# A routed two-layer network after attention: results added to the output rows tile by tile instead of in a last stage

## The reference

```
x      = x + attention(layernorm(x), ctx)
flat   = layernorm(x)                                   # rows the experts read
scores = softmax(flat @ router_weight.T + router_bias)  # T x 8
topk_vals, topk_idx = top_k(scores, 2)                  # two experts a token
gu     = flat @ gate_up_proj[e] + gate_up_bias[e]       # 512 -> 1024
gate   = minimum(gu[:512], 7);  up = clip(gu[512:], -7, 7)
act    = (up + 1) * gate * sigmoid(1.702 * gate)
down   = act @ down_proj[e] + down_bias[e]              # 512 -> 512
out    = x + sum over the token's two experts of topk_val * down
```

## Time and profile before

| | |
|---|---|
| median of 3 runs | 2001.87 us (1999.96 to 2002.34) |
| profiled execution, its own time | 2003.26 us |
| its span | 2001.5 us |
| mean granted TensorE clock | 0.933 of full speed |
| PE busy in the span | 1726.6 us (86%) |
| DVE busy | 1337.1 us (67%) |
| ACT busy | 667.1 us (33%) |
| POOL busy | 373.7 us (19%) |
| indirect gathers `xg` | 78 |
| indirect gathers `ya` | 64 |

### The profile page before, as it was taken

One profiled execution on the slowest core, in us unless ns is written; L12 is line 12 of the kernel. 1 busy time (PEld: TensorE's weight loads), 2 busy tenths in 40 slices (PEclk: granted clock), 3 DMA queues, 4 the chain that ended last, 5 costly groups with the idle time before them and its releaser, 6 DMA issues. The chain is left out here.

```text
span 2001.5 us, 31191 instructions
## 1 busy us (share of the span) xinstructions
PE 1726.6 (86%) x10594; PEld 1248.7 (62%) x10594; DVE 1337.1 (67%) x2380; ACT 667.1 (33%) x1108; POOL 373.7 (19%) x543
## 2 busy tenths in 40 slices
PE   6989999999899999998996389999999999999600
PEld 4547456365474563654743379898988988989500
DVE  3776776757767667577675766767677677776444
ACT  2341542623415326234153232424244244332100
POOL 3113013021130130211310111111111111110165
PEclk9999999999999999999998589999999999999855
DMA  6405216034062160340511413434354254421388
GB/s 213 115 1 167 67 38 195 2 89 144 1 170 64 39 194 2 96 138 1 148 44 43 169 32 106 150 104 148 108 178 159 96 190 155 162 85 54 116 290 297
DMA packets 111380, 228.70 MB, mean 114 GB/s; under 512 B 21232, under 2 KB 22256, under 8 KB 111216
## 3 DMA queue, kind: packets, MB, share of 16 engines
q1 hardware_dynamic: 85472, 162.40, 24.8%
q0 software_dynamic: 20576, 54.29, 9.3%
q10 hardware_dynamic: 5168, 9.96, 1.3%
HBM read 208.59 MB, written 45.61 MB: 127 GB/s over the span
## 5 line engine op out<-in xcount | busy, mean ns | idle before, releaser
L1205 PE MATMUL gu_ps<-xgT_hi,wg_hi 128*128 128x256 f32 x1248 | 356.3, 286 | 41.7 <-issue 40.1
L1205 PE MATMUL gu_ps<-xgT_hi,wg_lo 128*128 128x256 f32 x1248 | 353.8, 283 | 0.0
L1205 PE MATMUL gu_ps<-xgT_lo,wg_hi 128*128 128x256 f32 x1248 | 353.6, 283 | 0.0
L448 ACT ACTIVATE pt<-st 128x1024 f32<-128x1024 f32 x256 | 249.3, 1018 | 152.2 <-PE st L291 152.2
L1205 PEld LDWEIGHTS gu_ps<-xgT_hi,wg_hi 128*128 128x128 f32 x1248 | 243.2, 195 | 51.8 <-issue 51.2
L1205 PEld LDWEIGHTS gu_ps<-xgT_lo,wg_hi 128*128 128x128 f32 x1248 | 243.3, 195 | 0.7
L1205 PEld LDWEIGHTS gu_ps<-xgT_hi,wg_lo 128*128 128x128 f32 x1248 | 242.9, 195 | 0.0
L609 DVE TENSOR_REDUCE negmax<-work 128x1 f32<-128x512 f32 x256 | 174.9, 689 | 62.5 <-PE work L276 61.4
L1320 DVE TENSOR_SCALAR gate<-gu_ps,bg 128x256 f32<-128x256 f32 x156 | 75.3, 482 | 165.1 <-PE gu_ps L1205 165.1
L291 PE MATMUL st<-qs,ks 98*128 98x512 f32 x512 | 165.2, 416 | 5.9 <-ACT pt L448 5.2
L609 DVE TENSOR_REDUCE negmax<-st 128x2 f32<-128x1024 f32 x128 | 151.6, 1218 | 25.6 <-PE st L276 23.9
(11 more groups left out here) (174 smaller groups left out, 3023.1 us busy)
## 6 DMA issues: line engine op xcount, KB each, us to landing
raw_g<-w_gate_up SPq DMA_DIRECT2D x39, 2048.0 KB
raw_d<-w_down SPq DMA_DIRECT2D x39, 1024.0 KB
ks<-k_hi SPq DMA_DIRECT2D x256, 64.0 KB, 2.0
qs<-q_hi SPq DMA_DIRECT2D x256, 64.0 KB, 2.4
y_dram<-y SPq DMA_DIRECT2D x20, 512.0 KB, 3.2
bd<-b_down SPq DMA_DIRECT2D x39, 256.0 KB
y_dram<-y ACTq DMA_DIRECT2D x19, 512.0 KB, 2.8
x_in<-x SPq DMA_DIRECT2D x8, 1024.0 KB, 5.4
```

The lines of the kernel that those rows point to most:

```text
L448: e.activation(pt[k % 2][:, 2 * p:2 * p + 2, :], st[st_ring.bank[b, "exp", c, k, p]][:, :, :], ACT.Exp, scale=scale).then_inc(exped.sem, 1)
L1205: ins = e.matmul(gu_ps[n % GU_BANKS][:, part, :], wg[s][pw][:, k, cols], xgT[s][px][:, k, :], start=(k == 0 and m == 0), stop=(k == KD - 1 ...
```

## The change

- `combine_stage` is gone, with `y_dram`, `x2_dram`, `w12` and the `y` and `hid_f` tiles. The attention stage stores its residual rows into `out`.
- Rows of `xln_dram` get 8 more floats behind their 512: a DMA in the routing stage, first on SP's queue, writes there the token's weight for each expert (zero for those not chosen). The gather of a tile's rows brings them along, and `pick_weight` (two small VectorE instructions after `row_lo`) picks the tile's expert by `tile_hot`.
- `mix(i)` takes the place of `add_down_bias(i)`: four VectorE instructions of 128x512 (`scalar_tensor_tensor`): `acc = d_ps * w + acc` twice, then `acc = bd * w + acc` twice. It stands one turn later, after f = 1 of the next tile's parts, ahead of the `down_lo` and `gate_up_lo` there.
- GpSimd has in each turn: scatter `acc` of tile i - 1 to `out` (two indirect DMAs, each after its half is mixed), wait for them to land, fetch the rows of tile i + 3 (two), gather the rows of `out` for tile i into `acc` (two). The next `mix` waits for these.
- SP's load of the down bias waits for `mixed` of tile i; the stores of `y` on SP and ScalarE are gone.
- `hidden_lo(f - 2)` stands ahead of `clip(f)`, which now waits for it, as `hid_f` is kept in `up`.
- The routing stage has some 20 more small VectorE instructions and two matmuls after the token list, which give padding slots a token of their tile or a spare one.

```diff
@@ routing_stage
             e.wait_ge(exped, 1)
-            then(e.tensor_reduce(inv_sum[:, :], expo[:, :, :], AX.X, ALU.add))
-            last()
-            then(e.reciprocal(w12[:, 0, :], inv_sum[:, :]))
-            ...
+            then(e.tensor_reduce(exp_sum[:, :], expo[:, :, :], AX.X, ALU.add))
+            last()
+            then(e.tensor_tensor(weight[:, :, :], expo[:, :, :], hots[:, :, :], ALU.mult))
+            then(e.reciprocal(inv_sum[:, :], exp_sum[:, :]))
+            last()
+            then(e.tensor_tensor(weight[:, :, :], weight[:, :, :], e_of(inv_sum[:, :]), ALU.mult), "weight")
...
+            then(e.tensor_scalar(pad[:, :], token_1[:, :], 0.5, None, ALU.is_lt))
+            last()
+            e.wait_ge(first_sent, 1)
+            then(e.tensor_tensor(pad[:, :], pad[:, :], first_ps[:, :], ALU.mult))
+            ...
+            then(e.tensor_scalar(in_run[:, :], column(token_f, 0), part_f[:, 0:1], None, ALU.is_equal), "in_run")
+            e.wait_ge(run_made, 1)
+            ...
+            then(e.tensor_copy(token_of[:, :], token_f[:, :]))
...
         def on_sp(e):
+            e.wait_ge(vec, at["weight"])
+            e.dma_start(w_rows, weight[:, :, :]).then_inc(w_stored, 16)
             e.wait_ge(vec, at["tiles"])
             first_loads(e)
@@ expert_stage, TensorE
                         if k == 0 and i:
-                            e.wait_ge(y_made.sem, y_made[i - 1, j])
+                            e.wait_ge(y_added.sem, y_added[i - 1, j])
@@ expert_stage, VectorE
-            def add_down_bias(i):
+            def pick_weight(i):
+                e.wait_ge(gathered[i % 2], turn(i) * 16 * SUB)
+                ...
+                e.tensor_tensor(w_all[:, :, :], xg[i % 2][:, :, D:DX], tile_hot[:, i, :, :], ALU.mult).then_inc(w_made.sem, 1)
+                e.wait_ge(w_made.sem, w_made[i, "all"])
+                e.tensor_reduce(w_slot[i % WSL][:, :], w_all[:, :, :], AX.X, ALU.add).then_inc(w_made.sem, 1)
+
+            def mix(i):
                 s = i % 2
+                e.wait_ge(acc_in[s], turn(i) * 16 * SUB)
+                e.wait_ge(w_made.sem, w_made[i, "slot"])
+                for j in range(SUB):
+                    e.wait_ge(down_made.sem, down_made[i, j])
+                    e.scalar_tensor_tensor(out=acc[s][:, j, :], in0=d_ps[j][:, :], scalar=w_slot[i % WSL][:, j:j + 1], in1=acc[s][:, j, :],
+                                           op0=ALU.mult, op1=ALU.add).then_inc(y_added.sem, 1)
                 e.wait_ge(bd_in[s], turn(i) * 16)
                 for j in range(SUB):
-                    e.wait_ge(down_made.sem, down_made[i, j])
-                    if i >= 2:
-                        e.wait_ge(stored[s], 16 * (turn(i) - 1))
-                    e.tensor_tensor(y[s][:, j, :], d_ps[j][:, :], bd[s][:, :], ALU.add).then_inc(y_made.sem, 1)
+                    e.wait_ge(y_added.sem, y_added[i, j])
+                    e.scalar_tensor_tensor(out=acc[s][:, j, :], in0=bd[s][:, :], scalar=w_slot[i % WSL][:, j:j + 1], in1=acc[s][:, j, :],
+                                           op0=ALU.mult, op1=ALU.add).then_inc(mixed.sem, 1)
...
                     for f in range(KF):
+                        if f > 1:
+                            hidden_lo(now, f - 2)
                         clip(now, f)
                         if f:
                             glu(now, f - 1)
-                        if f > 1:
-                            hidden_lo(now, f - 2)
+                        if f == 1 and i >= 1:
+                            mix(i - 1)
                         if f % 2:
                             down_lo(now, f // 2, down_changed)
...
                 if i + 2 < n_tiles:
                     row_lo(i + 2)
-                if i >= 0:
-                    add_down_bias(i)
+                    pick_weight(i + 2)
+            mix(n_tiles - 2)
+            mix(n_tiles - 1)
@@ expert_stage, GpSimd
+            def fetch_sums(i):
+                s = i % 2
+                if i:
+                    e.wait_ge(scattered.sem, scattered[i - 1])
+                for j in range(SUB):
+                    e.indirect_dma_start(out=acc[s][:, j, :], out_offset=None, in_=out_rows, in_offset=slot_rows(i, j)).then_inc(acc_in[s], 16)
+
+            def store_sums(i):
+                for j in range(SUB):
+                    e.wait_ge(mixed.sem, mixed[i, j])
+                    e.indirect_dma_start(out=out_rows, out_offset=slot_rows(i, j), in_=acc[i % 2][:, j, :], in_offset=None).then_inc(scattered.sem, 16)
+
+            e.wait_ge(w_stored, 16)
             fetch(0)
             fetch(1)
-            for i in range(-1, n_tiles - 1):
+            fetch_sums(0)
+            for i in range(-1, n_tiles):
+                if i >= 1:
+                    store_sums(i - 1)
                 if i + 3 < n_tiles:
                     fetch(i + 3)
+                if i >= 1:
+                    fetch_sums(i)
+            store_sums(n_tiles - 1)
+            e.wait_ge(scattered.sem, scattered[n_tiles - 1])
@@ expert_stage, SP
                 if i >= 2:
-                    e.wait_ge(y_made.sem, y_made[i - 2, SUB - 1])
+                    e.wait_ge(mixed.sem, mixed[i - 2, SUB - 1])
```

More of the change, by code:

```diff
@@ L866, in routing_stage @@
     SLOTS = token_of.shape[1]
+    SUB = FTOK // P
     SHIFT = P.bit_length() - 1
@@ L911, in routing_stage @@
         low = sb("low", [P, SLOTS])
+        token_1 = sb("token_1", [P, SLOTS])
+        token_f = sb("token_f", [P, SLOTS])
+        pad = sb("pad", [P, SLOTS])
+        first = sb("first", [P, SLOTS])
+        empty = sb("empty", [P, n_tiles])
+        spare = sb("spare", [P, n_tiles])
+        in_run = sb("in_run", [P, n_tiles], BF16)
+        ones_row = sb("ones_row", [1, P])
         ended = sb("ended", [P, n_tiles, E])
@@ L1044, in on_dve @@
                 n_some = KT // NQ
-                tiles = slice(some.start % NT, some.start % NT + n_some)
+                tiles = slice(some.start % NT + 1, some.start % NT + n_some + 1)
                 last()
@@ L1079, in on_pe @@
             ins.then_inc(listed, 1)
+            e.wait_ge(consts_made, ONES_ROW)
+            e.wait_ge(vec, at["token_1"])
+            e.matmul(first_ps[:, :], ones_row[:, :], token_1[0:1, :], start=True, stop=True).then_inc(first_sent, 1)
+            e.wait_ge(vec, at["in_run"])
+            e.matmul(run_ps[:, :], ones_b[:, :], in_run[:, :], start=True, stop=True).then_inc(run_made, 1)
         def on_sp(e):
+            e.wait_ge(vec, at["weight"])
+            e.dma_start(w_rows, weight[:, :, :]).then_inc(w_stored, 16)
             e.wait_ge(vec, at["tiles"])
@@ L1116, in expert_stage @@
     GU_BANKS = 4
+    IDX, WSL = 4, 3
+    DX = D + E
     rows = xln_dram.rearrange("b s d -> (b s) d")
+    out_rows = out.rearrange("b s d -> (b s) d")
     tiles = range(n_tiles)
@@ L1130, in expert_stage @@
         bu1 = [sb(f"bu1{s}", [P, KF]) for s in range(2)]
-        idx = [sb(f"idx{s}", [P, SUB], I32) for s in range(2)]
-        xg = [sb(f"xg{s}", [P, SUB, D]) for s in range(2)]
+        idx = [sb(f"idx{s}", [P, SUB], I32) for s in range(IDX)]
+        xg = [sb(f"xg{s}", [P, SUB, DX]) for s in range(2)]
+        acc = [sb(f"acc{s}", [P, SUB, D]) for s in range(2)]
+        w_all = sb("w_all", [P, SUB, E])
+        w_slot = [sb(f"w_slot{s}", [P, SUB]) for s in range(WSL)]
         xgT = [pair("xgT", [P, KD, FTOK], s) for s in range(2)]
@@ L1136, in expert_stage @@
         up = [sb(f"up{i}", [P, FTOK]) for i in range(2)]
-        hid_f = [sb(f"hid_f{i}", [P, FTOK]) for i in range(2)]
         hid = [pair("hid", [P, KF, FTOK], s) for s in range(2)]
-        y = [sb(f"y{s}", [P, SUB, D]) for s in range(2)]
         t_ps = [psum(f"t_ps{i}", [P, 2, FTOK]) for i in range(KD // 2)]
@@ L1150, in expert_stage @@
         gathered = [sem(f"gathered{s}") for s in range(2)]
-        stored = [sem(f"stored{s}") for s in range(2)]
+        acc_in = [sem(f"acc_in{s}") for s in range(2)]
+        scattered = Mark(sem("scattered"), tiles, 16 * SUB)
+        w_made = Mark(sem("w_made"), [(i, n) for i in tiles for n in ("all", "slot")])
         of_f = [(i, f) for i in tiles for f in range(KF)]
@@ L1159, in expert_stage @@
         glu_made, hid_made, hid_lo_made = Mark(sem("glu_made"), of_f), Mark(sem("hid_made"), of_f), Mark(sem("hid_lo_made"), of_f)
-        y_made = Mark(sem("y_made"), [(i, j) for i in tiles for j in range(SUB)])
+        y_added = Mark(sem("y_added"), [(i, j) for i in tiles for j in range(SUB)])
+        mixed = Mark(sem("mixed"), [(i, j) for i in tiles for j in range(SUB)])
         idx_made = Mark(sem("idx_made"), tiles)
@@ L1373, in on_dve @@
             row_lo(0)
+            pick_weight(0)
             for i in range(-1, n_tiles):
@@ L1448, in on_sp @@
                     load_down_bias(i + 2)
-                if i >= 0 and i % 2 == 0:
-                    store(e, i)
-            for s in range(2):
-                e.wait_ge(stored[s], 16 * len(tiles[s::2]))
```

152 lines of the change are left out of this document (57 added, 95 removed).

## The result

The changed kernel takes 2017.83 us, the median of 4 runs (2016.04 to 2021.23); the kernel before took 2000.91 beside it. The ratio is 1.0088, 95% interval 1.007 to 1.0107: slower by 0.9%. The profiled execution took 2016.04 us; its span is 2014.3, against 2001.5 before, and its mean granted clock 0.942.

A forecast was written before the change was run, and what follows sets the result against it. It took PE to bound plain turns, VectorE's serial work turns with new weights, and GpSimd and DMA the 116 us combining stage. Terms: -103.1 + 92 + 3 + 6 + 5.7 = +3.6 us; forecast 2005 us, range 1968 to 2043.

The forecast's parts named there:

- three signs: Forecast wrong if plain turns exceed 18 us (loop), A and C don't slow the clock, or ScalarE waits for `raw_g`.
- the loop: Slower rival: GpSimd's round through DRAM (scatter, gather, landings) exceeds 17.6 us and decides; 2045 to 2053; chance 0.16.
- Routing, +5.7: Dependent steps and two PE trips behind the token list, two steps before it: 5.7 us, bounds 4 and 8.
- A, B and C: Three turns where an expert follows another: +2.75, +5.3, +3.1, turn behind C +2.0; 13.1 us, seven times: 92.
- The clock: Waits of about 3 us drop PE to the lower clock; 1.9 to 3.0 us of turn C are the clock's.
- The rival in which the clock does not follow: Faster: new waits of 2.6 to 3.8 us leave the clock alone; 8.6 a place, 1973; chance 0.24.
- The rival of late weights: Slower: weight loads share DMA engines badly, ScalarE waits in B too, 3 us at seven places: 2026; chance 0.10.
- SP: Down-bias load waits for `mixed` and delays weight loads: 1.2 us in A at five places, 6 us; B 0.
- Plain turns, the step that failed: Turns without new weights: VectorE's idle time absorbs most of `mix`; 0.3 us a turn, ten turns, 3 us.
- mix, 2.7 us: Four VectorE instructions about 0.68 apart, 2.7 us, bounds 2.6 and 3.0; serial addition with `clip`'s waits 2.9.
- GpSimd's chain, 15.5 us a round: Round from `mix` to `mix` through scatter and gather takes 15.5 us, below 17.6, so price 0.
- The end, 36.3 us: Last scatter lands 36.3 us behind the last `gate_up`, where the span ended 139.45 behind; gain 103.1 us.

The follow-up runs named there:

- the best version: Changed kernel with mix(i) behind row_lo, old order of hidden_lo and large tiles at multiples of 64 bytes: 1911.77 us, ratio 0.9566; with filling 1898.43 us, ratio 0.9488.
- the filling: Best version plus 14 identity matmuls whose result nobody reads ahead of gate_up of turn C, seven places: 1898.43 us, ratio 0.9488.
- The run with half the filling: Changed kernel plus 14, 24 and 10 identity matmuls ahead of gate_up behind turns A, B and C, seven places: 2013.18 us, ratio 1.005.
- the bias run: Changed kernel with SP's load of the down bias moved behind the weight loads: 2021.28 us, ratio 1.0097.
- without both: Changed kernel with half the filling and SP's down-bias loads behind the weight loads, both at once: 1985.45 us, ratio 0.9924.
- The order run: Changed kernel with hidden_lo(f - 2) back behind glu(f - 1) and its own hid_f tile, mix left in place: 2016.15 us, ratio 1.0074.
- the late `mix`: Changed kernel with mix(i) at the end of turn i, behind row_lo and pick_weight: 1923.32 us, ratio 0.9628.
- half a `mix` less: Changed kernel with the second pair of mix instructions (weighed down bias) left out: 1993.51 us, ratio 0.9948.
- the first aligned kernel: Changed kernel plus two unused 32-byte tiles, so every large expert-stage tile starts at a multiple of 64 bytes: 2016.52 us, ratio 1.0086.

## Why the prediction came out as it did

The forecast for the profiled execution was +3.6 us; it was +12.8, in the range (which was 75 us wide) and on the side that had the most weight, but outside the forecast's no change. That it came so near is in part luck: the steps below miss by 18.3 us on one side and by 9 on the other. The prediction also named three signs by which it would be wrong, and two of them came, the third in part. Plain turns are over 18 us, though not by the loop that the sign stood for; four of the seven C leave the clock alone; and ScalarE waits for `raw_g`, 30.7 us in seven waits, which the prediction's own term for late weights in A had foreseen, so that this sign contradicted the sum. By its steps:

*Routing, +5.7.* The first `gate_up` starts 5.4 later. Right.

*A, B and C.* The seven A grew by 26.0 us, forecast 23.2 (2.75 each, and 2.0 for the two that stand behind a C); B by 35.2, forecast 37; C by 20.6, forecast 22. The waits behind them were forecast at 3.8, 6 and 2.6 us and are 4.20, 6.26 and 2.77 at the first place, 3.3 to 4.2, 5.5 to 6.7 and 2.7 to 3.1 at the seven.

*The clock.* It fell behind all seven A (waits of 3.3 us and more) and all seven B. Behind C it was forecast to fall too, and did so three times in seven, at the first place and at two of the four shown here; the same wait of 2.77 us stands ahead of all these stretches but the third, which had 3.14:

```profile
1448.82:1452.82 4.00, 4.00 (x34) 4.00 (x35) 1.22 (x4) 0.38 (x1) 1.14 (x2) 1.00 0.61 188
1555.68:1559.68 4.00, 4.00 (x24) 4.00 (x25) 0.34 (x2) 1.06 (x1) 2.92 (x3) 0.68 0.84 269
1735.59:1739.59 4.00, 4.00 (x19) 4.00 (x20) 0.34 (x2) 1.06 (x1) 3.09 (x4) 0.50 0.79 257
1807.98:1811.98 4.00, 4.00 (x34) 4.00 (x35) 1.22 (x4) 0.38 (x1) 1.14 (x2) 1.00 0.74 188
```

At the first place, where it fell, the next turn took 20.0 us, where it did not, a plain turn's 18.75. The rival in which the clock does not follow was right for four of 21 waits; a wait of 2.77 us went either way.

The clock's share of C was read too high. The prediction took all that C has over 17.28 us for the clock's, 1.9 to 3.0 us (by the earlier trace rows it is 2.1 to 3.3). In another kernel, the best version, the filling took the lower clock away there, and C kept 0.5 to 1.0 us of it.

But the reason for B was half of it. The prediction had its 5.3 us from VectorE's work and the clock, and cost late weights in B at 0, "PE is late by then anyway". The run with half the filling took the clock away and B kept its length; the bias run took the late weights away and B kept 25.0 of 25.7 us. Only without both is it 23.5, 2.6 above the 20.9 of before, about the 2.65 us of work in `mix`; the other 2.5 are what the late weights and the clock cause together. VectorE by time in B of the changed kernel shows both at work in a row: a late first part, then a wait for `wg_hi` (the `row_lo` ahead of B first):

```profile
1288.84 1.29 DVE L1365 TENSOR_TENSOR xgT_lo<-t_ps,xgT_hi 128x512 fp32r<-128x512 f32 x2
...
1294.86 0.48 DVE L1373 TENSOR_SCALAR gate<-gu_ps,bg 128x256 f32<-128x256 f32 x1 [3.16 <-issue]
...
1297.26 1.23 DVE L1231 TENSOR_TENSOR wg_lo<-raw_g,wg_hi 128x1024 fp32r<-128x1024 f32 x1 [1.53 <-ACT wg_hi L1225]
```

Two causes that lie beside each other give one delay. The size was right because the one was hidden behind the other, which is luck where the prediction counted one of them and argued the other away. The rival of late weights was right in that ScalarE waits in B, and wrong in that this adds 3 us seven times.

*SP.* The times were right. The load of `raw_g` was forecast to be issued 13.2 us into its turn and to be used 3.5 to 5.5 us into A; it was issued at 1262.63, 13.28 in, and used at 1272.08, 3.96 into A:

```profile
1272.08 1.06 ACT L1225 ACTIVATE wg_hi<-raw_g 128x1024 fp32r<-128x1024 f32 x1 [4.89 <-DMA raw_g<-w_gate_up]
```

The price of 6 us in A was too high: the bias run took this wait away and the first A became 0.35 us shorter (at the later places other waits came in).

*Plain turns, the step that failed.* Forecast +0.3 us, measured +1.45. Over the fifteen turns outside A, B, C and the first two it makes +21.5, forecast 13 (ten times 0.3 and five times 2.0 behind C). Two terms were mis-sized. The move of `hidden_lo(f - 2)` ahead of `clip(f)` was taken for two pipeline ends of 0.1 us. What it does is put VectorE behind ScalarE: `hidden_lo` needs `hid_hi`, and the two instructions of `clip` that used to cover ScalarE's time now come after. VectorE by time in a plain turn:

```profile
1262.26 0.43 DVE L1388 TENSOR_TENSOR hid_lo<-up,hid_hi 128x256 fp32r<-128x256 f32 x1 [0.55 <-ACT hid_hi L1331]
...
1264.79 0.45 DVE L1380 TENSOR_TENSOR gate<-gate,sig 128x256 f32<-128x256 f32 x1 [0.33 <-issue]
```

The order run shows its size: with the old order a plain turn is 0.9 us shorter. But the order doesn't cost this alone. With the late `mix` and the new order six of the fifteen other turns are at 17.7 to 17.9 too (seven are still at 18.7 to 18.8), and half a `mix` less takes 0.33 us off: the 0.9 us are the new order and `mix` ahead of `row_lo` together, where the prediction had 0.3 for both. The second term was not in the prediction at all: TensorE's pace, 0.08 to 0.11 us for each of the four parts and 0.10 in `down`, some 0.5 us a turn. The two add up to 1.4 of 1.45. Why 2.80, 2.83 and 2.84 differ, and why the first aligned kernel kept 5.45 while the best version has 5.35, stays open.

*mix, 2.7 us.* Its four instructions took 2.65 to the start of the next. *pick_weight, nothing.* Right: it ends before VectorE's next wait.

*GpSimd's chain, 15.5 us a round.* 15.1 in a plain turn; nobody waited for it but the last two tiles.

*The end, 36.3 us.* 42.7. GpSimd and VectorE by time, in the last two tiles:

```profile
1994.56 1.26 POOL L1496 DMA_INDIRECT out<-acc,idx  x1 [5.28 <-DVE acc L1410]
...
1999.57 0.99 POOL L1491 DMA_INDIRECT acc<-out,idx  x1 [2.47 <-DMA out<-acc,idx]
...
2006.97 1.26 POOL L1496 DMA_INDIRECT out<-acc,idx  x1 [5.14 <-DVE acc L1410]
2008.53 0.99 POOL L1496 DMA_INDIRECT out<-acc,idx  x1 [0.30 <-issue]
```

```profile
1992.21 1.41 DVE L1405 SCALAR_TENSOR_TENSOR acc<-d_ps,w_slot,acc 128x512 f32<-128x512 f32 x2 [3.77 <-DMA acc<-out,idx]
...
2004.62 1.41 DVE L1405 SCALAR_TENSOR_TENSOR acc<-d_ps,w_slot,acc 128x512 f32<-128x512 f32 x2 [9.68 <-DMA acc<-out,idx]
```

The round from `mix(37)` to `mix(38)` is 12.4 us, forecast 11.2; ahead of it the first gather lands 20.6 behind the last `gate_up`, forecast 18.4; behind it the end is 9.7 away, forecast 6.7. In the last piece the prediction had the two scatters leave at the pace of `mix`, 0.7 apart. They leave at GpSimd's, 1.56 apart. The last lands at 2011.7, 3.2 us behind its issue and sooner than forecast, but the program ends 2.6 us later: the trace has a DRAIN instruction of GpSimd from 2011.91 to 2014.09, a term that the prediction did not have (before, the span ended 0.9 us behind the last transfer). 6.4 us in all.

So of the 9.2 us missed, 6.4 are the end. The rest is 8.5 too little for the fifteen plain turns and 2.8 for A, and too much for B and C (3) and for late weights in A (6; what they cost is in A's measured growth), with 0.6 more from the first two turns and routing.

**The rule of the skill.** The prediction weighed that VectorE instructions with two SBUF inputs and GpSimd's SBUF reads exclude each other, and said that most issues don't meet it. The trace of after agrees with the rule, in every first scatter of a pair. In a plain turn, in A, in B and in C:

```profile
1259.21 1.59 POOL L1496 DMA_INDIRECT out<-acc,idx  x1 [8.46 <-DVE acc L1410]
...
1278.41 2.73 POOL L1496 DMA_INDIRECT out<-acc,idx  x1 [8.84 <-DVE acc L1410]
...
1302.32 3.93 POOL L1496 DMA_INDIRECT out<-acc,idx  x1 [7.69 <-DVE acc L1410]
...
1328.34 2.80 POOL L1496 DMA_INDIRECT out<-acc,idx  x1 [12.24 <-DVE acc L1410]
```

Behind `mix`, VectorE runs on with instructions that read two SBUF tiles: `hidden_lo` in a plain turn, `gate_up_lo` ahead of it in A, `down_lo` in C, both in B. This run ends with `hid_lo`, and the issue 0.87 to 0.89 us behind it, in 37 of the 39 tiles. VectorE by time in B:

```profile
1302.63 1.28 DVE L1234 TENSOR_TENSOR wd_lo<-raw_d,wd_hi 128x512 fp32r<-128x512 f32 x2
1303.83 1.22 DVE L1231 TENSOR_TENSOR wg_lo<-raw_g,wg_hi 128x1024 fp32r<-128x1024 f32 x1
1304.96 0.42 DVE L1388 TENSOR_TENSOR hid_lo<-up,hid_hi 128x256 fp32r<-128x256 f32 x1
1305.49 0.48 DVE L1373 TENSOR_SCALAR gate<-gu_ps,bg 128x256 f32<-128x256 f32 x1
```

`hid_lo` ends at 1305.38 and the scatter's issue at 1306.25; in A 1280.27 and 1281.14; in C 1330.26 and 1331.14; in the plain turn 1259.94 and 1260.80. The Trainium skill says in "SBUF — State Buffer", section "SBUF: two separate sides", that one of the two gets the shared ports for a whole instruction and that the other blocks. The trace agrees and goes further: the issue is held up by VectorE's whole run of such instructions, one behind the other, and not by one of them. Two runs that changed what follows `mix` show the same. With the old order of `hidden_lo` the first scatter in a plain turn, in A, in B and in C took 1.25, 2.39, 3.59 and 2.46 us, 0.34 less each, and ended 0.87 us behind the last `mix`, `wg_lo` or `wd_lo` in place of `hid_lo`. With the late `mix`, behind which nothing of the kind follows, all 39 first ones took 1.25 or 1.26; there the second ones that start beside the next turn's `wg_lo` took 1.79, and ended 0.86 us behind it.

It cost no time that can be seen: a round of 15.1 us in a plain turn of 18.74 leaves GpSimd over 3 us to spare, and `mix` waits for its rows in the last two tiles alone.

## What to carry to other kernels

Work that is added ahead of the instruction an engine waits for costs its length, and then the clock behind the longer wait; the same work behind that instruction cost far less: 92 us lay in the place of four instructions, by estimate a third of them in what the longer wait and the later loads brought with them. Where two causes may hold the same turn, take both away at once: singly they gained nothing and 7.6 us, together 33. When an order of instructions is changed between engines that answer each other, look for what used to cover the round trip.

## What the hardware showed that was not expected

- The issue of an indirect scatter took 1.59, 2.73, 3.93 or 2.80 us by the VectorE instructions beside it, and ended 0.87 us behind the last of them; 1.00 us without them.
- Behind the last scatter's landing a program that ends on GpSimd took another 2.6 us, 2.2 of them a DRAIN.
- The pace of the same matmuls was 2.72, 2.80, 2.83 or 2.84 us for 24 and 5.35 or 5.45 for `down`, between kernels that differ in the addresses of SBUF tiles, and in one kernel between turns.
- 14 matmuls whose result nobody reads, in waits of 2.8 to 4.1 us at seven places, held the granted clock at 1.00 behind them and made a kernel faster, by 16 us of ratio (0.9488 against 0.9566) and 13 of median (1898.43 against 1911.77).
